# A two-layer graph kernel with gathered row tiles: row tiles 8, 10, 12 and 14 in place of 9, 11, 13 and 14, and the orders of all engines around them

## What is computed

```python
h = jnp.maximum(_layernorm(x), 0.0)                 # x: 2048 x 512, float32
# layer 0, "adj" is 2048 x 2048 with about 3 nonzeros a row, weight is 512 x 512
xq      = _act_quant(h, act_alpha, 4)
weight_q = _weight_quant((weight - mean) / std, wgt_alpha, 3)
support = relu(matmul(xq / act_delta, weight_q / wgt_delta) * act_delta * wgt_delta)
support_q = _act_quant(support, act_alpha2, 4)
x = x + matmul(adj / s, support_q / support_delta) * s * support_delta
# layer 1: attention over the pairs; for these inputs each softmax row has one
# entry, the diagonal, so that the layer adds its input
h = jnp.maximum(_layernorm(x), 0.0)
x = x + attention(h, adj, pairs)
```

## Time and profile before

| | us |
|---|---|
| median of 3 runs | 182.28 |
| the runs | 181.17, 182.28, 183.86 |
| the profiled execution | 180.63 |
| its span (first to last instruction) | 178.8 |
| PE, DVE, ACT, POOL busy | 128.4, 118.0, 95.3, 60.6 |
| mean granted TensorE clock | 0.884 |

### The profile page before, as it was taken

How to read it: one execution, slowest core, us unless ns; L and a number is a source line. 1 busy time by engine, 2 the same in 40 slices (tenths; PEclk the granted TensorE clock), 3 DMA queues, 4 the chain that set the end, 5 groups by cost and what they waited for, 6 DMA issues and landing times.

```text
span 178.8 us, 2002 instructions
## 1 busy us (share of the span) xinstructions
PE 128.4 (72%) x578; PEld 75.9 (42%) x582; DVE 118.0 (66%) x271; ACT 95.3 (53%) x145; POOL 60.6 (34%) x97
## 2 busy tenths in 40 slices
PE   0689992999899894990199079897399997006960
PEld 0664451455455443570036025564137574004950
DVE  0899980969996859998194064295386366977232
ACT  3787954468989440000580180792799949911000
POOL 2545332312630000001883004772787832321000
PEclk9999999699999999999669957999759999755795
DMA  5999999269969982006339507339649331111101
GB/s 183 400 398 402 406 401 271 69 178 235 307 150 230 321 342 63 0 8 133 134 102 271 201 0 264 103 103 306 269 120 291 127 111 59 59 59 59 62 4 62
DMA packets 18480, 32.45 MB, mean 182 GB/s; under 512 B 8033, under 2 KB 10850, under 8 KB 16930
## 3 DMA queue, kind: packets, MB, share of 16 engines
q1 hardware_dynamic: 17074, 28.48, 48.9%
q0 software_dynamic: 960, 2.36, 4.5%
q10 hardware_dynamic: 432, 1.44, 2.4%
HBM read 24.66 MB, written 6.30 MB: 173 GB/s over the span
## 4 chain that ended last, share of the span: by engine, by line
DVE 23%; DMA 19%; issue 18%; ACT 11%; POOL 11%; PE 9%; SPq 1%; POOLq 0%; DVEq 0%; ACTq 0%
DMA raw<-adj_t 14%; PE acc L1330 5%; ACT junk L564 5%; POOL narrow L834 4%; DVE st L1003 4%; DMA h_iT<-h_i 3%; DVE ring L1114 3%; POOL raw L819 3%; POOL rs L741 3%; DVE most L1061 3%; PE acc L1343 2%; DVE x_sb L1262 2%; ACT ring L613 2%; ACT h_i L583 2%; DVE lo L1055 2%
## 5 line engine op out<-in xcount | busy, mean ns | idle before, releaser
L1400 PE MATMUL acc<-sup_h,hi 128*128 128x512 f16 (+1 forms) x144 | 38.5, 435 | 19.0 <-ACT hi L556 18.3
L741 POOL TENSOR_TENSOR rs<-ve,minus_half 128x1 f32<-128x1 f32 (+2 forms) x21 | 16.9, 803 | 67.4 <-DVE ve L1014 67.2
L556 ACT ACTIVATE hi<-raw 128x2048 f16<-128x2048 f32 x7 | 13.3, 1905 | 43.1 <-DMA raw<-adj_t 43.1
L1406 PE MATMUL acc<-sup,lo 128*128 128x512 f32 (+1 forms) x144 | 33.1, 384 | 1.0 <-DVE lo L1055 1.0
L1400 PEld LDWEIGHTS acc<-sup_h,hi 128*128 128x128 f16 x144 | 16.2, 118 | 39.9 <-ACT hi L556 19.6
L1107 DVE TENSOR_TENSOR lo<-raw,hi 128x2048 fp32r<-128x2048 f32 x7 | 16.0, 2289 | 21.8 <-ACT hi L556 16.1
L1406 PEld LDWEIGHTS acc<-sup,lo 128*128 128x128 f32 x144 | 25.8, 197 | 6.2 <-DVE lo L1055 1.2
L564 ACT ACTIVATE junk<-raw,below 128x2048 uint8<-128x2048 f32 x12 | 23.8, 1987 | 0.0
L1348 PE MATMUL acc<-sup,lo 128*128 128x512 f32 x64 | 21.8, 452 | 0.0
L1003 DVE BATCH_NORM_STATS2 st<-x_sb 128x6 f32<-128x512 f32 x29 | 19.4, 685 | 0.4
L1330 PE MATMUL acc<-w_q,h_qT 128*128 128x512 bf16 x60 | 16.5, 397 | 4.3 <-DVE h_qT L1044 3.9
(11 more groups left out here) (117 smaller groups left out, 140.2 us busy)
## 6 DMA issues: line engine op xcount, KB each, us to landing
raw<-adj_t SPq DMA_DIRECT2D x11, 1024.0 KB, 7.4
raw<-adj_t SPq DMA_DIRECT2D x8, 512.0 KB, 11.0
out<-ring SPq DMA_DIRECT2D x15, 256.0 KB, 2.1
x_sb<-x SPq DMA_DIRECT2D x3, 1024.0 KB, 14.2
sup_d<-sup_h SPq DMA_DIRECT2D x16, 128.0 KB
w_sb<-weight SPq DMA_DIRECT2D x4, 258.0 KB, 3.9
raw<-adj_t ACTq DMA_DIRECT2D x1, 1024.0 KB
x_sb<-x SPq DMA_DIRECT2D x1, 512.0 KB, 5.7
```

What stands on the lines that cost most here:

```text
L741: nc.gpsimd.tensor_tensor(rs[:, a:a + m], ve[:, a:a + m], minus_half[:, 0:m], ALU.pow).then_inc(r_ready, 1)
L1400: nc.tensor.matmul(bank[:, cols], part(hi, k % PARTS, j), sup_h[:, j, cols], start=(j == 0), stop=False)
L1406: ins = nc.tensor.matmul(bank[:, cols], part(lo, k % PARTS, j), sup[:, j, cols], start=False, stop=(j == T - 1))
```

## The change

- **SPARSE** becomes (8, 10, 12, 14): gathered and dense tiles alternate from tile 8 on. Chunks 4 to 11 are now for the tiles 4, 5, 6, 7, 9, 11, 13, 15.
- **Pieces**: GpSimd subtracts pieces 10 to 19 as well as piece 0 (`POOL_LO`); VectorE keeps 1 to 9.
- **First results**: for tiles 0 to 3 GpSimd prepares `nm` = -rs and `nb` = mean x rs (`scaled`), ScalarE's relu scales by them, and GpSimd makes the four results (`first_out`) by a subtraction.
- **Sign**: for tiles 0 to 14, x1 is written negated (C_NEG in place of C_OUT, subtract in place of add), so that relu2 takes the mean as its bias with a scale of -1, and VectorE no longer writes `nm` after each tile; result subtracts x_sb instead of adding it.
- **sup_d** is stored in four parts of 512 KB behind the transposes of stage one, instead of 16 of 128 KB between them.
- **Loads**: ScalarE's queue loads halves 4 to 7 (j = 12, 13). SP loads chunk 5 right behind the last transpose, chunk 6 ahead of the last part of sup, chunks 7 and 8 ahead of turn_lists, chunk 9 ahead of the first result's store, and then one per step. ScalarE screens two chunks ahead of its loop over s.
- **Gathers**: the first stands ahead of all of GpSimd's steps s; the others follow the inverse root of step 6, 8 and 10.
- **VectorE** does the subtraction of chunk 5 ahead of the search and of chunk 6 behind it, and results one step later in its loop start with s = 5.
- **Flag**: TensorE's small matmul and VectorE's copy of the flag stand behind tile 15.
- Constants for the lists are made earlier on GpSimd, by one more instruction; the code for more than one batch of lists is gone.

```diff
-SPARSE = (9, 11, 13, 14)
+SPARSE = (8, 10, 12, 14)
...
+    POOL_LO = [0] + list(range(10, 4 * (GT + 1)))
+    VECTOR_LO = [p for p in range(4 * (GT + 1)) if p not in POOL_LO]
...
@@ sync @@
+            load_adj(GT + 1)
             sp.dma_start(sup_d[0:1, :], sup_h[0:1, 0, :]).then_inc(sup_stored, 16)
-            load_half(6)
-            store_sup(T - TURN)
-            load_adj(GT + 1)
-            store_sup(T - TURN + 1)
-            load_half(7)
-            for j in range(T - TURN + 2, T):
-                store_sup(j)
-            for n in range(min(S, NB + LATE)):
+            for g in range(3):
+                store_sup(g)
+            load_adj(GT + 2)
+            store_sup(3)
+            for n in range(S):
                 load_own(n)
-            turn_lists(0)
-            nxt = GT + 2
+            load_adj(GT + 3)
+            load_adj(GT + 4)
+            turn_lists()
+            nxt = GT + 5
@@ scalar @@
             def relu2(t):
-                act.wait_ge(centred, second_no(t))
...
+                if t < GT:
+
+                    act.wait_ge(scaled, 2)
+                    nc.scalar.activation(ring[:, t % RING, :], x_sb[:, t, :], ACT.Relu, bias=nb[:, t:t + 1],
+                                         scale=nm[:, t:t + 1]).then_inc(yp_ready, 1)
@@ gpsimd @@
+            for p in POOL_LO[1:]:
+                lo_of_piece(p)
...
+            gather_rows(0)
+            gather_sup(0)
+            gathered = 1
             for s in range(GT, T):
                 a, m = second_ln[s - GT]
                 pool.wait_ge(var_ready, FIRST - EARLY + 1 + s - GT)
                 inverse_root(a, m)
-                while gathered < S and SPARSE[gathered] <= s + LOOK + 1:
+                if s == GT:
+                    pool.wait_ge(r_ready, FIRST + 1)
+                    nc.gpsimd.tensor_scalar(nm[:, 0:GT], rs[:, 0:GT], -1.0, None, ALU.mult).then_inc(scaled, 1)
+                    nc.gpsimd.tensor_tensor(nb[:, 0:GT], mv[:, 0:GT, 0], rs[:, 0:GT], ALU.mult).then_inc(scaled, 1)
+                    for t in range(GT):
+                        pool.wait_ge(yp_ready, t + 1)
+                        nc.gpsimd.tensor_tensor(ring[:, t % RING, :], ring[:, t % RING, :], x_sb[:, t, :],
+                                                ALU.subtract).then_inc(first_out, 1)
+                if gathered < S and SPARSE[gathered] - s <= 4:
                     gather_rows(gathered)
                     gather_sup(gathered)
                     gathered += 1
@@ tensor @@
             for t in range(GT, T):
-                if t == T - 1:
-                    pe.wait_ge(row_counted, 1)
-                    pe.wait_ge(x1_ready, 9)
-                    nc.tensor.matmul(acc[0][:, 0:1], ones[:, :], ones_row[:, 1:2], start=True, stop=True).then_inc(flag_sum, 1)
                 if t in SPARSE:
                     aggregate_picked(t)
                 else:
                     aggregate(t)
+            pe.wait_ge(row_counted, 1)
+            pe.wait_ge(x1_ready, 9)
+            nc.tensor.matmul(acc[0][:, 0:1], ones[:, :], ones_row[:, 1:2], start=True, stop=True).then_inc(flag_sum, 1)
```

More of the change, by code:

```diff
@@ L204, in gnn_kernel @@
         beyond_ready = sem("beyond_ready")
-        at_out = [sem(f"at_out{b}") for b in range(BATCHES)]
-        at_in = [sem(f"at_in{b}") for b in range(BATCHES)]
+        at_out = sem("at_out")
+        at_in = sem("at_in")
         sup_stored = sem("sup_stored")
@@ L213, in gnn_kernel @@
         wide_ready = sem("wide_ready")
-        centred = sem("centred")
+        scaled = sem("scaled")
+        first_out = sem("first_out")
         half_ready = sem("half_ready")
@@ L333, in wait_lo, with base_at @@
             if k <= GT:
-                wait_lo_piece(eng, 4 * k + 3)
-                if k == 0:
-                    eng.wait_ge(lo_by_pool, 1)
+                for p in range(4 * k, 4 * k + 4):
+                    wait_lo_piece(eng, p)
             else:
                 eng.wait_ge(lo_ready, k - GT)
+        def base_at(i):
+            return base[:, 1 + S + i:2 + S + i]
         def ordinal(t):
@@ L670, in _ @@
                     seen += 1
+                if j in (12, 13):
+                    for n in (2 * j - 20, 2 * j - 19):
+                        load_half(act, n)
                 if j == T + 1:
                     split_hi(GT + 1)
+            for _ in range(2):
+                screen_ones(seen)
+                seen += 1
             for s in range(GT, T):
@@ L847, in _ @@
                     gathered += 1
+            assert gathered == S
             pool.wait_ge(last_var, 1)
@@ L1287, in _ @@
                     split_rest(SPARSE.index(s + 2))
-                for t in range(a, a + m):
-                    result(t)
+                result(s - 1)
                 if s + 2 == T:
                     dve.wait_ge(screened, ND)
-                    dve.wait_ge(beyond_ready, 2 * BATCHES + 1)
-                    nc.vector.tensor_scalar(beyond[:, 0:BATCHES], beyond[:, 0:BATCHES], 1.0, None, ALU.is_ge)
+                    dve.wait_ge(beyond_ready, 3)
+                    nc.vector.tensor_scalar(beyond[:, 0:1], beyond[:, 0:1], 1.0, None, ALU.is_ge)
                     nc.vector.tensor_reduce(ones_row[:, 2:3], low[:, :], AX_X, ALU.min)
@@ L1377, in aggregate_picked @@
                         nc.tensor.matmul(bank[:, cols], high[:, n % 2, j * P:(j + 1) * P],
[L1378 removed]
+                                         narrow[:, n, j * D + cols.start:j * D + cols.stop], start=False, stop=False)
                     pe.wait_ge(rest_ready, n + 1)
[L1380 removed]
+                    nc.tensor.matmul(bank[:, cols], rest[:, n, own], sup[:, t, cols], start=False, stop=False)
                     pe.wait_ge(wide_ready, n + 1)
                     for j in range(BLOCKS):
[L1383 removed]
+                        ins = nc.tensor.matmul(bank[:, cols], rest[:, n, j * P:(j + 1) * P],
                                                wide[:, n % WIDE, j * D + cols.start:j * D + cols.stop],
```

280 lines of the change are left out of this document (122 added, 158 removed).

## The result

| | before | after |
|---|---|---|
| median, us | 182.42 (181.17 to 183.86) | 168.02 (167.73 to 170.08) |
| ratio | | 0.923, 95% interval 0.913 to 0.933 |
| the profiled execution, its span | 180.63, 178.8 | 167.91, 166.1 |
| mean granted clock | 0.884 | 0.928 |

The kernel is 7.7% faster. The forecast was 165.5, its range 160.5 to 174. Between the profiled executions 12.7 us are gained, where the sum had 16.8. Some executions of any kernel here are 1.5% or more above the fastest of the same kernel; the medians count all executions, the ratios leave such ones out.

The account below looks back on a forecast made before the run. It took a ring of loads waiting for results, results for split chunks and splits for loads as the bound. Five terms sum to -16.8 us: 180.63 becomes 163.8, plus 1.65 to the median gives 165.5 us, range 160.5 to 174.

Parts of the forecast that it names:

- (1): Tiles 4 to 6: tile 4 still starts at 63.44, three dense tiles follow without waits, ending at 85.2; -12.9 us.
- (2): Tile 7: its split waits behind relus and GpSimd's first gather, so it ends at 102.7; +1.4 us.
- (3): Tile 7's end to tile 11's result: three gathered and dense pairs at 12.6 us each; -0.6 us.
- (4): Tile 11's result to the last: no flag wait before tile 15, VectorE's chain last, 16.9 us instead of 22.8; -5.9 us.
- (5): Ends: flag copied and read only after the last result, 0.9 us, and two flags in a row, 0.3; +1.2 us.
- I take 0, because TensorE's steps leave VectorE more than 1 us of room between a support and its use: Stage one: GpSimd's ten pieces holding VectorE's short steps cost nothing, within bounds of 0 to 11.6 us.
- the flags in a row: Stage one: two halves flagged in a row at j = 11 delay TensorE by 0.3 us.
- that rival: Stage one held by the shared port: GpSimd's pieces delay VectorE's steps by up to 11.6 us, 167 to 177; chance 0.1.
- GpSimd slower in the ring: Gathered and dense pairs: landings of 6.4 us and gathers of 8.8 lengthen the ring, 172 to 174 us; chance 0.2.
- the pieces set the pace: Stage one: slow GpSimd pieces fix its end; 2% slower from 3.7 us a piece, 189 us at 4; chance 0.03.
- within 1 us of 63.4: Sign for the forecast, at the end of stage one: tile 4 starts within 1 us of 63.4.
- I am wrong if tile 4 starts after 66: Sign against the forecast, at the end of stage one: tile 4 starting later than 66 us.

Follow-up runs that it names:

- a1: The changed kernel with pieces 10 to 19 subtracted on VectorE again instead of GpSimd: 166.57 us, ratio 0.911 to the kernel before.
- the two families of kernels: Five kernels with pieces 10 to 19 on GpSimd and flags in a row (tile 4 starts at mean 67.6 us), four with them on VectorE (64.5).
- b4: The kernel before, with SP loading chunk 6 ahead of the lists and every later chunk one step earlier: 171.91 us, ratio 0.944.
- c4: The changed kernel with ScalarE splitting tile 7's chunk ahead of the relus of tiles 0 to 3: 167.84 us, ratio 0.916 to the kernel before.
- b2: The changed kernel with the root and scaled numbers for tiles 0 to 3 between the first gather's two halves: 167.79 us, ratio 0.921 to the kernel before.
- b3: The changed kernel with each VectorE result made one step later in its order: 162.03 us, ratio 0.889 to the kernel before.
- b1: The changed kernel with tiles 9, 11, 13, 14 gathered as before the change, its orders kept: 167.83 us, ratio 0.925 to the kernel before.
- a4: The kernel before with tiles 8, 10, 12, 14 gathered, nothing else changed: 176.77 us, ratio 0.966.
- a3: The kernel before with TensorE's flag matmul and VectorE's copy of the flag behind tile 15: 178.43 us, ratio 0.971.

## Why the prediction was right, and where it was not

The forecast of 165.5 missed the median of 168.02 by 2.5 us. That is closer than the sum was: it gave 163.8 for the profiled execution, and that took 167.91, 4.1 us more. The 1.65 us added for the distance from that execution to the median belonged to the kernel before; in the changed kernel the distance is 0.1, so 1.5 us of the error cancelled by luck. By the same points in the two profiled executions:

| term | forecast | measured |
|---|---|---|
| (1) tiles 4 to 6 | -12.9 | -9.0 (98.1 to 89.1) |
| (2) tile 7 | +1.4 | +1.2 (16.1 to 17.3) |
| (3) tile 7's end to the result of tile 11 | -0.6 | -0.3 (38.5 to 38.2) |
| (4) to the last result | -5.9 | -6.2 (22.8 to 16.6) |
| (5) ends | +1.2 | +1.6 (3.3 to 4.9) |
| sum | -16.8 | -12.7 |

**(1) is the term that was mis-sized**, by 3.9 us, and all of it lies ahead of tile 4. From tile 4 to the end of tile 6 it took 21.9 us, as forecast (21.8). The step that failed is "I take 0, because TensorE's steps leave VectorE more than 1 us of room between a support and its use". A piece of 1.19 us on GpSimd turns VectorE's 0.42 and 0.28 us into 1.37 and 1.24, and two of those in a row are more than the room. a1 and the two families of kernels put it at some 3.1 us, within the bounds of 0 to 11.6 that the text kept. The rest of the 3.8 us is within the scatter of tile 4's start (63.1 to 65.9 with the orders of before); for the flags in a row, which I had at 0.3, no cost is shown. I had read the lock in one direction, weighed a rule that says it holds in both, and gave it a chance of 0.1. In the end the forecast and that rival both happened.

That loads behind results caused the holes at tiles 6 and 7 is shown by b4. It also shows that a few lines which issue loads earlier give 10 to 11 us alone, where the whole change gives 14.

**(2) was right as a time and wrong as a cost.** The lists, the gather and the wait at tile 7 came as worked out. But I let the rest of the kernel start from tile 7's end. c4 removed the hole and b2 halved it, and neither gained anything that can be measured. GpSimd's chain runs past it: first gather, the root, relus, four results (4.93 us), a root held to 2.62 by VectorE's subtraction, result, x1, statistics, second gather.

**(3) was right by its number and wrong by its ring.** The prediction closed it over ScalarE: widening, screening, relu, split, screening, relu, 12.6 us a pair. (Its own terms, a landing of 3.5, gathers of 8.0 and 2 us for meetings, come to 12.75.) The periods are 13.7 and 12.8, but the ring is that of GpSimd and VectorE: b3 changed only VectorE's order and broke it. That the term agrees to 0.3 us is luck: two different rings happen to be about as long. Of 12.8 us, 8.4 are the gather (118.37 to 126.75) and 4.4 two roots, a result, x1 and statistics. The landing that I took at 3.5 is 2.7 and is no step of this ring; it counts again in b3, where this ring is open. "The alternation by itself brings little" holds in the changed kernel (b1) and not in the one before (a4), where it is worth 6 us. b4 alone gives 10 to 11, a4 6 and a3 5, together some 22 us, and the changed kernel has 14. That the three take away parts of the same waits is the reading that fits (a4 shortened the flag's by 4 us, a3 removed it); no run combined them.

**(4)** is confirmed by a3 (16.7 us in its trace, 16.6 in the changed kernel's), **(5)** was 0.4 too small: from the last result's end (161.2) to the end of the span it is 4.9 us.

Of the rivals, the one with GpSimd slower in the ring didn't come (landings 2.7, not 6.4), nor did the pieces set the pace: they took 1.19 us. Of what was to show it, tile 4 "within 1 us of 63.4" failed, and "I am wrong if tile 4 starts after 66" came true; the time stayed in range because the terms behind came out as forecast, the third by luck. TensorE was not without a hole in stage one either (1.68 us ahead of 52.24, for VectorE). The other signs came or nearly came: ScalarE waited for narrow 2.4 to 3.7 us, three times; no wait at the flag's matmul; VectorE last by 6.6 us (161.2 against 154.6); SP's last chunk was issued at 103.8, not by 102.

What stays open is the first gap, between the first and second gather, which no run took apart in full, and how much of (5) is the flag's read by SP.

## What to carry to other kernels

The longest wait of the busiest engine need not cost anything: ask what else would have been late, and remove it alone to see. Where two engines exchange small results (a root here, a statistic there) and one of them has a block of long instructions in its queue, look for work that the other does behind the exchange though it was ready before; to move that ahead gave 6 us for four lines. Gains of edits that remove parts of one wait don't add up, and an edit's worth in the old order need not be its worth in the new (the alternation: 6 us in a4, none in b1).
